# An attention kernel: the adjacency mask is turned by transposing DMA transfers instead of TensorE, and widened by GpSimd instead of ScalarE

## The chip, the cores and the metric

The kernel runs on one core of a Trainium2 chip. The metric is the time of the core on the device in microseconds (us). Three runs of the kernel before are given by their median.

## The reference

One pre-norm graph attention layer with a residual, over 16 batch elements of 512 rows and 512 features, with 16 heads of 32. The mask `adj` is an int32 matrix of zeros and ones per batch element, 512 x 512, mostly zeros.

```python
h = jnp.maximum(_layernorm(x, axis=-1), 0.0)
q, k, v = heads(h @ Wq + bq), heads(h @ Wk + bk), heads(h @ Wv + bv)
scores = jnp.einsum('bhqd,bhkd->bhqk', q, k) * scale
scores = jnp.where(mask[:, None] == 0, -jnp.inf, scores)
attn = jax.nn.softmax(scores, axis=-1)
out = jnp.einsum('bhqk,bhkd->bhqd', attn, v)
x + out.transpose(0, 2, 1, 3).reshape(b, s, D_MODEL) @ Wo + bo
```

## The kernel before

**Two passes over the scores.** For each batch element and head the scores are made twice. Pass 1 has queries on the partitions: TensorE writes a tile of 128 queries x 512 keys (line 822), VectorE adds the mask and takes the row's extreme (608), ScalarE takes the exponential and its sum (444). This gives the softmax's correction c per query. Pass 2 has keys on the partitions: TensorE writes 128 keys x 512 queries with c already inside (834), ScalarE takes the exponential into `probs` (484), then VectorE (622, 625) or GpSimd (359) sets the masked elements to zero, and TensorE multiplies by v (852). A batch element has 64 tiles in either pass: four groups of heads, times four tiles of queries or keys, times four heads.

**The mask in two forms.** `bias_q` has queries on the partitions and holds 0 or -2^100 as bf16; VectorE forms it from `adj_tile`, four tiles per batch element (538). Pass 2 needs the mask with keys on the partitions: `bias_k` (the same numbers, for key tiles 0 and 2) and `keep_k` (int32 one or zero, for key tiles 1 and 3). Each is in two halves, one per pair of key tiles. To get a half, TensorE transposes eight 128x128 pieces of `bias_q` into a PSUM bank (778), and ScalarE copies the first four to `bias_k` (501) and widens the other four to `keep_k` (503). This is the turn called "m".

**The schedule.** Every engine runs the same program of blocks `k`, each of 64 slots `u`. In a slot TensorE does one tile of pass 1 (of block k or k-1), one of pass 2 (tile n = u + 4 of batch element k-1; from u = 60 on, tile u - 60 of batch element k), some of the products of the projections (758), in every fourth slot the product with v, and the turns which the table `TURNS` names: "h" (the transposes of the normalised rows, 772), "c" (783) and "m". Turns and pass-1 tiles share a ring of three PSUM banks, in the order of `RING`; before TensorE writes an entry it waits until the entry that last used this bank has been read. The m turns stand at u = 53 (half 0) and at u = 3 of the next block (half 1).

**SP's queue.** SP issues nearly all DMAs, in program order, each behind its own waits: the loads of x, of adj (`load_adj`, u = 17, 24, 30, 36), of y (the residual's rows) and the stores of y, and `load_stack`: twelve pieces of 32x512 that copy q or k from `part_hi` and `part_lo` into three row ranges of `q_stack` or `k_stack`. The stack loads stand at u = 33, 37, ..., 61 and at u = 1 of the next block; k of group 2 is at u = 49, q of group 3 at u = 61, k of group 3 at u = 1. They are called the k2, q3 and k3 loads here. Behind the k3 load stand, for batch element k-2, the store of y tile 0 (u = 5), the load of y tile 2 into the same buffer (u = 7), which waits for that store, then the store of tile 1 and the load of tile 3.

**GpSimd's program.** It masks tiles 4, 5, 6, 12, 13, 14 and 15 of each group of 16 in pass 2 (359), adds the bias row to the y tiles (350; the third y tile at u = 8, directly behind mask 12 and ahead of masks 13, 14 and 15), and computes the layer norm's scales. The product with v at u = 14 needs tiles 12 to 15 of group 0 masked.

## Time and profile before

| | us |
|---|---|
| median of 3 runs | 1663.86 |
| lowest and highest of them | 1663.39, 1666.87 |
| the profiled execution's own time | 1666.74 |
| its span in the trace | 1664.9 |
| TensorE busy in the span | 1602.4 |
| mean granted TensorE clock | 0.989 of full speed |

The span runs from the first to the last recorded instruction of the profiled execution; its own time is what a run measures. A block lasts about 100 us. The granted clock is given as a share of 2.4 GHz. Times in the timeline are from the span's start.

### The profile page before, as it was taken

Reading aid. Unit: us, or ns where it says so; the run is one execution under the profiler, and the core shown is the slowest. Engines: PE = TensorE matmul, PEld = TensorE weight load, DVE = VectorE, ACT = ScalarE, POOL = GpSimd, SP = SyncE. Lnnn points to the kernel's source line nnn. Section 1 sums busy time; section 2 is a strip of 40 time slices with the busy share of each in tenths; the row PEclk is TensorE's granted clock in tenths of the full one; section 3 lists DMA queues with packets and bytes.
Section 4 is the critical chain, followed back from the end, with each engine's and each line's share of the span. In section 5 each row is a group of like instructions: output and inputs, shape, how many; then the busy total and the mean of one; then the engine's idle time right before and its main releaser. Section 6 shows DMA issues by size and latency. Waiting matters only on the chain.

```text
span 1664.9 us, 27600 instructions
## 1 busy us (share of the span) xinstructions
PE 1602.4 (96%) x7745; PEld 1030.2 (62%) x7745; DVE 1440.1 (86%) x3504; ACT 1457.6 (88%) x3500; POOL 709.9 (43%) x641
## 2 busy tenths in 40 slices
PE   6799999999999999999999999999999999999987
PEld 4556666666666666666666666666666666666643
DVE  4889889888888989889898889989889898888885
ACT  3699899989999989899988998989898989999994
POOL 2044443543443544444453443544443443443442
PEclk9799999999999999999999999999999999999998
DMA  6434343433434344343433434344343434433320
GB/s 208 104 91 114 96 119 87 122 90 114 117 89 126 86 122 115 96 116 90 121 91 116 120 90 120 88 122 112 96 118 84 123 92 118 119 84 104 90 75 26
DMA packets 117168, 175.17 MB, mean 105 GB/s; under 512 B 30861, under 2 KB 32921, under 8 KB 117017
## 3 DMA queue, kind: packets, MB, share of 16 engines
q1 hardware_dynamic: 112536, 171.83, 37.8%
q10 hardware_dynamic: 4480, 1.58, 0.4%
q8 instruction: 64, 1.05, 0.3%
q14 instruction: 88, 0.71, 0.1%
HBM read 54.79 MB, written 16.78 MB: 43 GB/s over the span
## 4 chain that ended last, share of the span: by engine, by line
PE 83%; DVE 6%; ACT 4%; issue 4%; SPq 2%; DMA 1%; ACTq 0%; DVEq 0%
PE psP L758 37%; PE ps L822 16%; PE psO L852 13%; PE ps L834 13%; ACT ps L444 2%; DVE ps L608 2%; SPq L233 2%; PE ps L772 2%; DVE probs L622 1%; PE ps L778 1%; ACT bias_k L501 1%; ACT probs L484 1%; ACT keep_k L503 1%; DVE neg_max L608 0%; DMA q_stack<-part_hi 0%
## 5 line engine op out<-in xcount | busy, mean ns | idle before, releaser
L608 DVE CUSTOM_DVE_ANT_0 ps<-ps,bias_q 128x512 f32<-128x512 f32 x1024 | 708.6, 693 | 174.3 <-PE ps L822 167.1
L359 POOL TENSOR_TENSOR probs<-probs,keep_k 128x512 int32<-128x512 int32 x438 | 565.4, 1311 | 678.3 <-ACT probs L484 676.7
L444 ACT ACTIVATE ps<-ps,neg_max 128x512 f32<-128x512 f32 x1024 | 685.1, 669 | 115.2 <-DVE neg_max L608 92.9
L484 ACT ACTIVATE probs<-ps 128x512 f32<-128x512 f32 x1024 | 618.4, 604 | 16.8 <-PE ps L834 14.2
L822 PE MATMUL ps<-k_stack,q_stack 96*128 96x512 f32 x1024 | 453.2, 443 | 34.9 <-ACT ps L444 29.5
L834 PE MATMUL ps<-q_stack,k_stack 98*128 98x512 f32 x1024 | 411.5, 403 | 6.0 <-ACT probs L484 3.6
L622 DVE SCALAR_TENSOR_TENSOR probs<-bias_k,probs 128x512 f32<-128x512 bf16 x512 | 380.3, 743 | 3.4 <-ACT probs L484 3.2
L822 PEld LDWEIGHTS ps<-k_stack,q_stack 96*128 96x128 f32 x1024 | 193.2, 189 | 300.1 <-ACT ps L444 194.7
L852 PE MATMUL psO<-probs,v_sb 128*32 128x512 f32 x2048 | 275.4, 609 | 4.5 <-ACT probs L484 1.5
L834 PEld LDWEIGHTS ps<-q_stack,k_stack 98*128 98x128 f32 x1024 | 195.6, 191 | 45.3 <-ACT probs L484 17.4
L444 ACT ACTIVATION_READ_ACCUMULATOR ps<-ps,neg_max 128x1 f32 x1024 | 214.5, 210 | 0.0
L608 DVE DVE_READ_ACCUMULATOR2_ANT neg_max<- 128x1 f32 x1024 | 143.6, 140 | 0.0
L336 POOL TENSOR_SCALAR mean_var<-mean_var 128x1 f32<-128x1 f32 x64 | 14.5, 227 | 233.7 <-DVE mean_var L524 233.5
L758 PE MATMUL psP<-wv_hi,hT_hi 128*128 128x512 f32 x256 | 102.2, 399 | 1.1 <-DVE hT_lo L560 1.1
L758 PE MATMUL psP<-hT_hi,wq_hi 128*128 128x512 f32 x256 | 102.4, 400 | 0.7 <-DVE hT_lo L560 0.7
L758 PE MATMUL psP<-hT_lo,wq_hi 128*128 128x512 f32 x256 | 102.2, 399 | 0.0
L758 PE MATMUL psP<-hT_hi,wk_hi 128*128 128x512 f32 x256 | 101.7, 397 | 0.4 <-DVE wk_lo L572 0.3
L758 PE MATMUL psP<-wv_hi,hT_lo 128*128 128x512 f32 x256 | 101.8, 398 | 0.0
L758 PE MATMUL psP<-wv_lo,hT_hi 128*128 128x512 f32 x256 | 101.8, 398 | 0.0
L758 PE MATMUL psP<-hT_hi,wq_lo 128*128 128x512 f32 x256 | 101.7, 397 | 0.0
L852 PEld LDWEIGHTS psO<-probs,v_sb 128*32 128x32 f32 x2048 | 41.4, 108 | 97.2 <-issue 66.5
L758 PE MATMUL psP<-hT_lo,wk_hi 128*128 128x512 f32 x256 | 101.2, 395 | 0.0
(79 smaller groups left out, 1998.3 us busy)
## 6 DMA issues: line engine op xcount, KB each, us to landing
q_stack<-part_hi SPq DMA_DIRECT2D x512, 64.0 KB, 2.0
k_stack<-part_hi SPq DMA_DIRECT2D x504, 64.0 KB, 2.0
x_tile<-in_x_dram SPq DMA_DIRECT2D x66, 256.0 KB, 3.0
adj_tile<-in_adj_dram SPq DMA_DIRECT2D x64, 256.0 KB, 3.0
q_stack<-part_lo SPq DMA_DIRECT2D x256, 64.0 KB, 2.0
k_stack<-part_lo SPq DMA_DIRECT2D x256, 64.0 KB, 2.0
y_tile<-in_x_dram SPq DMA_DIRECT2D x62, 256.0 KB, 2.9
out_dram<-y_tile SPq DMA_DIRECT2D x62, 256.0 KB, 2.1
```

The source lines that it names most:

```text
L233: queue.dma_start(stack[row:row + 32, g, j, :].bitcast(F32), part[32 * j:32 * j + 32, i % 2, :].bitcast(F32)).then_inc(stack_in[kind], 16)
L359: nc.gpsimd.tensor_tensor(bits, bits, keep_k[:, kt // 2, :], ALU.mult).then_inc(gpsimd_masked, 1)
L444: nc.scalar.activation(item, item, ACT.Exp, scale=-1.0, bias=neg_max[:, g % 2, col:col + 1], accum_out=exp_sum[:, col:col + 1]).then_inc(e ...
L484: nc.scalar.activation(probs[:, n % P_RING, :], ps2[:, n % 2, :], ACT.Exp, scale=SCALE).then_inc(exp2_done, 1)
L501: nc.scalar.activation(bias_k[:, n, :], turned[:, 0:S], ACT.Identity).then_inc(bias_k_done, 1)
L608: nc.vector.tensor_tensor_reduce(bank1(("s", u)), bank1(("s", u)), bias_q[:, qt, :], -SCALE, 3.0e38, ALU.add, ALU.min, neg_max[:, g % 2, c ...
L622: nc.vector.scalar_tensor_tensor(out=tile, in0=bias_k[:, kt // 2, :], scalar=-MASKED, in1=tile, op0=ALU.add, op1=ALU.min).then_inc(vector_ ...
L758: last = nc.tensor.matmul(acc, w_l if i == 2 else w_h, m_l if i == 1 else m_h, start=(kt == 0 and i == 0), stop=(kt == NT - 1 and i == 2))
L772: last = nc.tensor.transpose(bank[:, P * t:P * t + P], x_view(b, n)[:, P * t:P * t + P], ident[:])
L822: nc.tensor.matmul(bank1(("s", u)), q_stack[0:STACK, g, j, P * qt:P * qt + P], k_stack[0:STACK, g, j, :], start=True, stop=True).then_inc( ...
L834: nc.tensor.matmul(ps2[:, n % 2, :], k_stack[:, g, j, P * kt:P * kt + P], q_stack[:, g, j, :], start=True, stop=True).then_inc(scores2, 1)
L852: last = nc.tensor.matmul(psO[32 * j:32 * j + 32, :], v_sb[:, (4 * b + kt) % 6, at:at + DH], probs[:, (4 * n + j) % P_RING, :], start=(kt ...
```

## The change

The m turns go. In their place SP issues four transposing DMAs per half (`turn_mask`), at u = 53 for half 0 and u = 61 for half 1: each takes 128 queries x 256 keys of `bias_q` and writes two blocks of 128 keys x 128 queries into the new tensor `turned`. Planes 0 and 1 of `turned` are `bias_k`; planes 2 and 3 share their memory with `adj_tile`, and GpSimd widens them into `keep_k` (`form_keep`, at u = 62 for half 0, at u = 6 of the next block for half 1). The adj loads wait until both widenings before them are done, and the transposes of a half wait until the masks that read the old half are done. The k2 load moves from u = 49 to u = 54, behind the first four transposes. The ring of PSUM banks has 72 entries in place of 74.

```diff
--- before.py
+++ after.py
@@ -46,8 +46,8 @@
 QK_ORDER = [x for x in TILES if x[0] in "qk"]
 
 
-TURNS = {1: [("h", 0, 0)], 3: [("m", 1, -1)], 5: [("h", 1, 0)], 8: [("c", 1, -1)], 10: [("h", 2, 0)], 13: [("h", 3, 0)],
-         24: [("c", 2, -1)], 40: [("c", 3, -1)], 53: [("m", 0, 0)], 56: [("c", 0, 0)]}
+TURNS = {1: [("h", 0, 0)], 5: [("h", 1, 0)], 8: [("c", 1, -1)], 10: [("h", 2, 0)], 13: [("h", 3, 0)],
+         24: [("c", 2, -1)], 40: [("c", 3, -1)], 56: [("c", 0, 0)]}
 
 
 RING = []
@@ -90,9 +90,10 @@
         oT_hi = sb("oT_hi", [P, NT, S], F32R)
         oT_lo = sb("oT_lo", [P, NT, S], F32R)
         x_tile = sb("x_tile", [P, NT, D], F32)
-        adj_tile = sb("adj_tile", [P, S], I32)
+        turned = sb("turned", [P, NT, S], BF16)
+        bias_k = turned[:, 0:2, :]
+        adj_tile = turned[:, 2:4, :].rearrange("p a s -> p (a s)").bitcast(I32)
         bias_q = sb("bias_q", [P, NT, S], BF16)
-        bias_k = sb("bias_k", [P, NT // 2, S], BF16)
         keep_k = sb("keep_k", [P, NT // 2, S], I32)
         probs = sb("probs", [P, P_RING, S], F32)
         part_hi = sb("part_hi", [P, 2, S], F32R)
@@ -138,7 +139,7 @@
         var_done, rstd_done, norm_done = sem("var_done"), sem("rstd_done"), sem("norm_done")
         h_turned, h_hi_done, h_lo_done = sem("h_turned"), sem("h_hi_done"), sem("h_lo_done")
         bias_done = sem("bias_done")
-        m_turned, bias_k_done, m_done = sem("m_turned"), sem("bias_k_done"), sem("m_done")
+        m_in, keep_done = [sem("m_in0"), sem("m_in1")], sem("keep_done")
         qkv_done, out_done = sem("qkv_done"), sem("out_done")
         qk_hi_done, qk_lo_done = sem("qk_hi_done"), sem("qk_lo_done")
         v_done = sem("v_done")
@@ -259,8 +260,20 @@
                     row = 4 * b + t
 
                     sp.wait_ge(bias_done, due(4 * b + t))
-                    sp.dma_start(adj_tile[:], adj_rows[bass.ds(row, 1)].rearrange("a p d -> (a p) d")
+                    sp.wait_ge(keep_done, due(2 * b))
+                    sp.dma_start(adj_tile, adj_rows[bass.ds(row, 1)].rearrange("a p d -> (a p) d")
                                  ).then_inc(adj_in, 16)
+
+            def turn_mask(b, half):
+
+                if have(b):
+                    sp.wait_ge(bias_done, 4 * b + 4)
+                    sp.wait_ge(keep_done, due(2 * b - 1 + half))
+                    sp.wait_ge(vector_masked, due(vector_before(64 * (b - 1) + 48 + 8 * half + 8)))
+                    sp.wait_ge(gpsimd_masked, due(gpsimd_before(64 * (b - 1) + 48 + 8 * half + 8)))
+                    for t in range(NT):
+                        sp.dma_start_transpose(turned[:, half::2, P * t:P * t + P],
+                                               bias_q[:, t, 2 * P * half:2 * P * half + 2 * P]).then_inc(m_in[half], 16)
 
             def load_y(b, t):
                 if have(b):
@@ -293,8 +306,9 @@
                     if u in (7, 11) and k - 2 != LAST: load_y(k - 2, (u + 1) // 4)
                     if u in (44, 46): load_y(k - 1, (u - 44) // 2)
                     if u in (48, 50) and k - 1 == LAST: load_y(LAST, (u - 44) // 2)
-                    if u % 4 == 1:
-                        done = tile_at(k, u // 4 - 1) if u >= 4 else tile_at(k - 1, 15)
+                    if u in (53, 61): turn_mask(k, (u - 53) // 8)
+                    if u % 4 == 1 and u != 49 or u == 54:
+                        done = tile_at(k, u // 4 - 1 - (u == 54)) if u >= 4 else tile_at(k - 1, 15)
                         if done and done[0] in "qk" and done != ("k", 0, 0):
                             load_stack(sp, done[2], QK_ORDER.index(done[:2]))
                         if done == ("k", 0, 0):
@@ -353,13 +367,24 @@
             def mask(b, n):
                 kt = n % 16 // 4
                 if n < 16 and n % 4 == 0:
-                    pool.wait_ge(m_done, due(2 * b + kt // 2 + 1))
+                    pool.wait_ge(keep_done, due(2 * b + kt // 2 + 1))
                 pool.wait_ge(exp2_done, due(64 * b + n + 1))
                 bits = probs[:, n % P_RING, :].bitcast(I32)
                 nc.gpsimd.tensor_tensor(bits, bits, keep_k[:, kt // 2, :], ALU.mult).then_inc(gpsimd_masked, 1)
 
+            def form_keep(b, half):
+
+                if have(b):
+                    pool.wait_ge(m_in[half], 64 * (b + 1))
+                    pool.wait_ge(vector_masked, due(vector_before(64 * (b - 1) + 48 + 8 * half + 8)))
+                    pool.wait_ge(gpsimd_masked, due(gpsimd_before(64 * (b - 1) + 48 + 8 * half + 8)))
+                    nc.gpsimd.tensor_scalar(keep_k[:, half, :], turned[:, 2 + half, :], -1.0 / MASKED, 1.0, ALU.mult, ALU.add
+                                            ).then_inc(keep_done, 1)
+
             def step(k, parity):
                 for u in range(SLOTS):
+                    if u == 62: form_keep(k, 0)
+                    if u == 6: form_keep(k - 1, 1)
                     b, n = pass2(k, u)
                     if have(b) and on_gpsimd(b, n):
                         mask(b, n)
@@ -493,15 +518,6 @@
                                 act.wait_ge(qkv_done, due(12 * k))
                             nc.scalar.activation(hT_hi[:, :, P * n:P * n + P], bank1((kind, n, rel)).rearrange("p (t q) -> p t q", q=P),
                                                  ACT.Relu).then_inc(h_hi_done, 1)
-                        if kind == "m" and have(k + rel):
-                            b = k + rel
-                            act.wait_ge(m_turned, due(2 * b + n + 1))
-                            turned = bank1((kind, n, rel)).bitcast(BF16)
-                            act.wait_ge(vector_masked, due(vector_before(64 * (b - 1) + 48 + 8 * n + 8)))
-                            nc.scalar.activation(bias_k[:, n, :], turned[:, 0:S], ACT.Identity).then_inc(bias_k_done, 1)
-                            act.wait_ge(gpsimd_masked, due(gpsimd_before(64 * (b - 1) + 48 + 8 * n + 8)))
-                            nc.scalar.activation(keep_k[:, n, :], turned[:, S:2 * S], ACT.Identity,
-                                                 scale=-1.0 / MASKED, bias=1.0).then_inc(m_done, 1)
 
             blocks(step, first=0)
 
@@ -532,10 +548,11 @@
             def form_bias(b, t):
 
                 if have(b):
-                    dve.wait_ge(m_turned, due(2 * b))
+                    dve.wait_ge(m_in[0], due(64 * b))
+                    dve.wait_ge(m_in[1], due(64 * b))
                     dve.wait_ge(masked_max, due(64 * (b - 1) + 48 + 4 * t + 4))
                     dve.wait_ge(adj_in, due(16 * (4 * b + t + 1)))
-                    nc.vector.tensor_scalar(bias_q[:, t, :], adj_tile[:], 0.0, MASKED, ALU.is_equal, ALU.mult
+                    nc.vector.tensor_scalar(bias_q[:, t, :], adj_tile, 0.0, MASKED, ALU.is_equal, ALU.mult
                                             ).then_inc(bias_done, 1)
 
             def form_c(b, g):
@@ -613,9 +630,9 @@
 
                         kt = n % 16 // 4
                         if n < 16 and kt % 2 == 0:
-                            dve.wait_ge(bias_k_done, due(2 * b + kt // 2 + 1))
+                            dve.wait_ge(m_in[kt // 2], due(64 * (b + 1)))
                         elif n < 16:
-                            dve.wait_ge(m_done, due(2 * b + kt // 2 + 1))
+                            dve.wait_ge(keep_done, due(2 * b + kt // 2 + 1))
                         dve.wait_ge(exp2_done, due(64 * b + n + 1))
                         tile = probs[:, n % P_RING, :]
                         if kt % 2 == 0:
@@ -711,8 +728,6 @@
                     if kind == "h":
                         pe.wait_ge(h_hi_done, due(4 * b + n + 1))
                         pe.wait_ge(h_lo_done, due(4 * b + n + 1))
-                    elif kind == "m":
-                        pe.wait_ge(m_done, due(2 * b + n + 1))
                     else:
                         pe.wait_ge(c_rows_done, due(4 * b + n + 1))
                     return
@@ -771,13 +786,6 @@
                     for t in range(NT):
                         last = nc.tensor.transpose(bank[:, P * t:P * t + P], x_view(b, n)[:, P * t:P * t + P], ident[:])
                     last.then_inc(h_turned, 1)
-                elif kind == "m":
-                    pe.wait_ge(bias_done, due(4 * b + 4))
-                    for i in range(2 * NT):
-                        key_tile, t = 2 * n + i // NT, i % NT
-                        last = nc.tensor.transpose(bank[:, 64 * i:64 * i + 64].bitcast(BF16),
-                                                   bias_q[:, t, P * key_tile:P * key_tile + P], ident_b)
-                    last.then_inc(m_turned, 1)
                 else:
                     pe.wait_ge(c_lo_done, due(4 * b + n + 1))
                     nc.tensor.transpose(bank[0:32, 0:P], c_parts[:].rearrange("p a n -> p (a n)").bitcast(F32), ident[:]
```

On SP the change adds instructions and moves one load. These are SP's instructions from the load of y tile 1 to the load of y tile 2 in one block, first as they were (`part_hi` and `part_lo` to `k_stack` or `q_stack` are the stack loads, each in twelve pieces; the names in brackets are the semaphores waited on):

```order
L273 DMA y_tile<-in_x_dram 128x512 [waits y_out1]
L233 DMA k_stack<-part_hi 32x512 [waits qk_hi_done,scores2]
...
L233 DMA k_stack<-part_lo 32x512 [waits qk_lo_done]
...
L233 DMA q_stack<-part_hi 32x512 [waits qk_hi_done,scores2]
...
L233 DMA k_stack<-part_hi 32x512 [waits qk_hi_done,scores2]
...
L280 DMA out_dram<-y_tile 128x512 [waits y_done]
L273 DMA y_tile<-in_x_dram 128x512 [waits y_out0]
```

And these are the same now:

```order
L286 DMA y_tile<-in_x_dram 128x512 [waits y_out1]
L275 DMA_TRANSPOSE turned<-bias_q 128x2x128 [waits vector_masked,gpsimd_masked,keep_done,bias_done]
L275 DMA_TRANSPOSE turned<-bias_q 128x2x128 x3
L234 DMA k_stack<-part_hi 32x512 [waits qk_hi_done,scores2]
...
L234 DMA k_stack<-part_lo 32x512 [waits qk_lo_done]
...
L275 DMA_TRANSPOSE turned<-bias_q 128x2x128 [waits vector_masked,gpsimd_masked,keep_done,bias_done]
L275 DMA_TRANSPOSE turned<-bias_q 128x2x128 x3
L234 DMA q_stack<-part_hi 32x512 [waits qk_hi_done,scores2]
...
L234 DMA k_stack<-part_hi 32x512 [waits qk_hi_done,scores2]
...
L293 DMA out_dram<-y_tile 128x512 [waits y_done]
L286 DMA y_tile<-in_x_dram 128x512 [waits y_out0]
```

Four transposes stand ahead of the k2 load and four between it and the q3 load. The k3 load, the store of y tile 0 and the load of y tile 2 follow as before.

GpSimd's instructions around the seam of two blocks, from masks 12 to 15 of the last group on, before:

```order
L359 TENSOR_TENSOR probs<-probs,keep_k 128x512 [waits exp2_done] x4
L359 TENSOR_TENSOR probs<-probs,keep_k 128x512 [waits exp2_done,m_done]
L359 TENSOR_TENSOR probs<-probs,keep_k 128x512 [waits exp2_done] x2
L359 TENSOR_TENSOR probs<-probs,keep_k 128x512 [waits exp2_done,m_done]
L350 TENSOR_TENSOR y_tile<-y_tile,bo_row 128x512 [waits y_in0]
L359 TENSOR_TENSOR probs<-probs,keep_k 128x512 [waits exp2_done] x3
```

And now:

```order
L373 TENSOR_TENSOR probs<-probs,keep_k 128x512 [waits exp2_done] x4
L381 TENSOR_SCALAR keep_k<-turned 128x512 [waits gpsimd_masked,vector_masked,m_in0]
L373 TENSOR_TENSOR probs<-probs,keep_k 128x512 [waits exp2_done,keep_done]
L373 TENSOR_TENSOR probs<-probs,keep_k 128x512 [waits exp2_done] x2
L381 TENSOR_SCALAR keep_k<-turned 128x512 [waits gpsimd_masked,vector_masked,m_in1]
L373 TENSOR_TENSOR probs<-probs,keep_k 128x512 [waits exp2_done,keep_done]
L364 TENSOR_TENSOR y_tile<-y_tile,bo_row 128x512 [waits y_in0]
L373 TENSOR_TENSOR probs<-probs,keep_k 128x512 [waits exp2_done] x3
```

One widening stands ahead of mask 4 and one ahead of mask 12; the addition of the bias row keeps its place.

## Rows read from the trace of the kernel before

**Rows 1.** The page, busy time, share of the span and instructions of each engine.

```profile
PE 1602.4 (96%) x7745; PEld 1030.2 (62%) x7745; DVE 1440.1 (86%) x3504; ACT 1457.6 (88%) x3500; POOL 709.9 (43%) x641
```

**Rows 2.** The page, the chain that ended last, shares by engine.

```profile
PE 83%; DVE 6%; ACT 4%; issue 4%; SPq 2%; DMA 1%; ACTq 0%; DVEq 0%
```

**Rows 3.** Timeline of PE at slot 53: start, length, engine, line, what [idle before].

```profile
960.95 0.63 PE L778 MATMUL ps<-ident,bias_q 128*128 128x128 bf16 x8
961.39 0.48 PE L822 MATMUL ps<-k_stack,q_stack 96*128 96x512 f32 x1
...
962.02 1.06 PE L852 MATMUL psO<-probs,v_sb 128*32 128x512 f32 x8
963.42 0.50 PE L822 MATMUL ps<-k_stack,q_stack 96*128 96x512 f32 x1 [0.34 <-ACT ps L444]
```

**Rows 4.** Timeline of PE, slots 3 and 4 of the next block.

```profile
983.08 0.63 PE L778 MATMUL ps<-ident,bias_q 128*128 128x128 bf16 x8
983.52 0.48 PE L822 MATMUL ps<-k_stack,q_stack 96*128 96x512 f32 x1
...
984.54 0.40 PE L758 MATMUL psP<-wo_hi,oT_lo 128*128 128x512 f32 x1
984.77 0.40 PE L758 MATMUL psP<-wo_hi,oT_hi 128*128 128x512 f32 x1
985.55 0.50 PE L822 MATMUL ps<-k_stack,q_stack 96*128 96x512 f32 x1 [0.38 <-ACT ps L444]
```

**Rows 5.** Timeline of PE, the product with v of slot 14.

```profile
1000.93 1.07 PE L852 MATMUL psO<-probs,v_sb 128*32 128x512 f32 x8
1001.93 0.50 PE L822 MATMUL ps<-k_stack,q_stack 96*128 96x512 f32 x1
```

**Rows 6.** Timeline of POOL: masks 62 and 63, 4 and 5, y tile 2, masks 13-15.

```profile
970.32 2.64 POOL L359 TENSOR_TENSOR probs<-probs,keep_k 128x512 int32<-128x512 int32 x2 [0.82 <-ACT probs L484]
979.14 2.54 POOL L359 TENSOR_TENSOR probs<-probs,keep_k 128x512 int32<-128x512 int32 x2 [6.17 <-ACT probs L484]
...
993.82 1.28 POOL L350 TENSOR_TENSOR y_tile<-y_tile,bo_row 128x512 f32<-128x512 f32 x1 [0.22 <-DMA y_tile<-in_x_dram]
995.05 3.78 POOL L359 TENSOR_TENSOR probs<-probs,keep_k 128x512 int32<-128x512 int32 x3
```

**Rows 7.** Timeline of SP's queue, from the q3 load to y tile 2.

```profile
972.78 2.41 SPq L233 DMA_DIRECT2D q_stack<-part_hi  x4
...
985.37 2.49 SPq L233 DMA_DIRECT2D k_stack<-part_hi  x4
988.02 0.45 SPq L280 DMA_DIRECT2D out_dram<-y_tile  x1
990.20 0.34 SPq L273 DMA_DIRECT2D y_tile<-in_x_dram  x1
```

**Rows 8.** Timeline: VectorE's masks 55 and 0, ScalarE's k3 part.

```profile
959.19 0.69 DVE L625 SCALAR_TENSOR_TENSOR probs<-keep_k,probs 128x512 f32<-128x512 int32 x1
...
973.36 0.69 DVE L622 SCALAR_TENSOR_TENSOR probs<-bias_k,probs 128x512 f32<-128x512 bf16 x1
...
977.80 0.70 ACT L468 ACTIVATE part_hi<-psP,cols 128x512 fp32r<-128x512 f32 x1
```

**Rows 9.** Timeline of PE, the idle that ends at 42.41.

```profile
42.41 0.76 PE L822 MATMUL ps<-k_stack,q_stack 96*128 96x512 f32 x1 [3.82 <-issue]
```

**Rows 10.** Windows of one us: stretch, its length, busy (count) per engine, PEclk, DMA, GB/s.

```profile
42.00:43.00 1.00, 0.59 (x2) 0.53 (x3) 1.00 (x2) 0.00 (x0) 0.00 (x0) 0.71 0.34 59
43.00:44.00 1.00, 1.00 (x4) 0.81 (x3) 1.00 (x1) 0.00 (x0) 0.00 (x0) 0.50 0.79 264
44.00:45.00 1.00, 1.00 (x4) 0.81 (x3) 1.00 (x3) 0.00 (x0) 0.00 (x0) 0.50 0.51 135
45.00:46.00 1.00, 0.73 (x2) 0.01 (x1) 1.00 (x4) 0.27 (x1) 0.00 (x0) 0.59 0.27 66
```

**Rows 11.** DMA issues: target and source, count, KB each, median us to landing.

```profile
k_stack<-part_hi SPq DMA_DIRECT2D x504, 64.0 KB, 2.0
```

## The prediction

> **What bounds the kernel now.** I read the page first: engine totals, clock and chain. TensorE is busy 96% of the span, ScalarE 88%, VectorE 86%, GpSimd 43% [rows 1], and 83% of the chain that ended last is TensorE's own work [rows 2]. So a microsecond taken from TensorE, or a microsecond in which it waits, is one of the result. Work taken from ScalarE counts only where TensorE waits for it.
>
> Then the timeline of one block, k=10, because the schedule repeats every 64 slots. At slot 53 the eight transposes of the mask begin at 960.95 and the next score at 961.39; the score of slot 54 then starts with 0.34 of idle before it, released by the ScalarE exponential that stood behind the two mask copies [rows 3]. The same at slot 3: 983.08 to 983.52, and 0.38 idle before 985.55 [rows 4]. What the reader should see is that a mask turn costs twice: its own time, and a bank that comes free late.
>
> **What the change takes away.** The transposes: 961.39 - 960.95 and 983.52 - 983.08, so 0.44 each. The waits: the rows draw a matmul longer than the step to the next one (984.54 to 984.77 is 0.23 [rows 4]; eight narrow products start 1.00 before their successor, 1000.93 to 1001.93 [rows 5]). So the waits are 985.55 - 984.77 - 0.23 = 0.55 and 963.42 - 962.02 - 1.00 = 0.40. Per batch 0.44 + 0.55 + 0.44 + 0.40 = 1.83, over 16 batches **-29.3 us**. It is an upper end: it holds if ScalarE, freed of two copies per turn, has nothing else behind. The lower end is the transposes alone, 16 x 0.88 = 14.1. I take 29.3, because both rows name ScalarE as the releaser and the copies stand directly before that exponential. The smaller ring (72 entries for 74) changes which bank is used and not how many entries lie between two uses, except at the block's seam, where two become three: nothing, or a little gained.
>
> **What it adds on GpSimd.** 32 widenings. No row shows this form; the nearest are its masks, 2.64 for two [rows 6], so 1.3 each. The first follows mask 63, which ends at 972.96, and the next mask comes at 979.14 after 6.17 of idle; the second stands two slots before mask 12. I cost them at nothing. If that cover were gone, GpSimd's masks would start up to 1.3 later.
>
> **What it adds on SP, the term that decides.** Eight transposing DMAs per batch, four per half. The order matters. The four of the first half stand ahead of the k2 stack load (12 pieces), which moves from slot 49 to 54. The four of the second half stand ahead of the q3 load and, behind it, the k3 load, the store of y tile 0 and the load of y tile 2. All of this is one queue, and it is a full one: from 972.78 to 987.86 SP issues 24 pieces without a gap, 0.63 each; then the store at 988.02 and, when that has landed, the load at 990.20 [rows 7]. GpSimd's addition of the bias row waits for that load (0.22 idle, start 993.82), and masks 13, 14 and 15 stand behind it on GpSimd and end at 998.83 [rows 6]. TensorE's fourth product with v needs all three and starts at 1000.93 [rows 5]. So the slack from SP to TensorE is 1000.93 - 998.83 = 2.1 now, and 1.1 once the turn of slot 3 (0.99) is gone.
>
> Let X be the time for which one transposing DMA holds SP. No row shows one. The lower end is SP's cheapest issue, 0.34 for a load of 128 partitions [rows 7]. The upper end is 2.5: a stack piece, also from SBUF to SBUF, takes 0.63 for 32 partitions, and this one has 128 of them. I take X = 1.0, nearer to the stack piece, since the cost of an issue plainly doesn't follow partitions (the load of 128 is the cheaper of the two), but above it, since a transpose must cut its data into more parts.
>
> The first half may start when mask 55 is done on VectorE, 959.19 + 0.69 = 959.9 [rows 8]; later events move 0.84 forward with the turn of slot 53 gone, so on their clock this is 960.7. Plus 4X is 964.7, plus 12 x 0.63 is 972.2. The second half waits for mask 63 on GpSimd, 970.32 + 2.64 = 972.96 [rows 6], so it isn't late, and q3 starts at 972.96 + 4.0 = 977.0 in place of 972.78: SP is 4.2 later. Nothing in the chain behind it has room, so masks 13 to 15 end at 1003.0, TensorE is ready at 999.9, and it stands still for 4.2 - 1.1 = 3.1. This happens in the 15 blocks that load y tile 2 there: **+46.5 us**.
>
> A stop of this length has a second price. After TensorE's idle of 3.82 before 42.41 the granted clock was 0.71, 0.50, 0.50 and 0.59 in the four microseconds from 42 to 46, half of full speed, the lower of its two levels (1.2 and 2.4 GHz) [rows 9, 10]. The clock lost there is 0.29 + 0.50 + 0.50 + 0.41 = 1.7 us. Between none and 1.7 per stop I take 1.7, because 3.1 is nearer to 3.82 than to the idles of under half a microsecond in rows 3 and 4: **+25.5 us**.
>
> What I cost at nothing: the mask itself is in time. The first half lands at 964.7 + 2.0 (the stack piece's landing [rows 11]), and VectorE first needs it at 973.36 [rows 8]. The second half is issued by 977.0, lands near 979, and is needed after 985.5 [rows 4]. The k2 load lands near 974.2, and ScalarE needs it at 977.80 [rows 8]. The adjacency loads, which now wait for the second widening, come about 15 us later.
>
> **Sum**, against the profiled execution's own time of 1666.7: 1666.7 - 29.3 + 46.5 + 25.5 = 1709.4. The median of the runs is 2.9 lower, so the forecast is **1707**.
>
> A rule speaks against the change. By the table of the Trainium skill, "VectorE: DVE Perf Modes", section "The three transpose paths", one 128x128 bf16 transpose costs 1309 ns by DMA and 390 on TensorE; the trace has eight in 0.44, far below that second figure. If its 1.31 were X, the second half would start at 973.4, q3 at 978.7, the stop would be 4.8, and the time 1666.7 - 29.3 + 15 x 6.5 = 1735, or 1732 against the median.
>
> **Rivals.**
> (a) *A transposing DMA holds SP no longer than a stack piece.* X = 0.63: q3 starts at 975.5, 2.7 late, the stop is 1.6, taken as too short for the clock: 1666.7 - 29.3 + 24 = 1661.4, or 1658.5 against the median, faster. With X = 0.34 the stop is 0.5 and the result 1642. The point from which it decides is where 15 stops equal 29.3, a stop of 1.95, so X = 0.72. For it: issues of 128 partitions at 0.34. Against it: both transfers inside SBUF are the dearer ones. Chance 0.22 for faster, and 0.06 for landing within 0.2% of no change. The Trainium skill says the same in "Advanced Engine Details and Errata", section "X-Bar Transpose (TRN2)": transposing DMAs are as fast as regular ones. No row of this trace shows one.
> (b) *It holds SP longer than 1.2.* Then SP reaches the second half late as well, and each further 0.1 of X costs 0.8. X = 1.5: q3 at 980.3, 7.5 late, a stop of 6.4 plus 1.7, so 1666.7 - 29.3 + 15 x 8.1 = 1759, or 1756 against the median. At 2.5 the stop is 14.4 and the time near 1880. For it: 16-bit elements must be split far finer than rows of 2 KB. Chance 0.17 for an X over 1.3 (above 1732), of it 0.09 above 1756.
> (c) *The stop comes, but the clock holds.* 1666.7 - 29.3 + 46.5 = 1684, or 1681 against the median; 0.2 of the chances, inside those of the forecast's case.
>
> The forecast's case (X from 0.75 to 1.3, with or without the clock) has 0.55. Faster 0.22, within 0.2% (about what a measurement of this kernel can tell from no change) 0.06, slower 0.72. The range goes from 1642, the cheapest issue, to 1756, X = 1.5; about 0.12 is left out. The forecast's case alone would be 1666 to 1732.
>
> **What would show it.** In the timeline of SP: the four transposes' steps (X), q3 starting at about 977 by block 10's clock, no gap from there to the store of y tile 0. In GpSimd's: the addition of the bias row preceded by some 4 us of waiting for the y load, directly before three masks. In TensorE's: no L778, no idle in slots 4 and 54, and one stop of about 3 us before the fourth product with v in each of 15 blocks, with the granted clock at half behind it. The forecast is wrong if X is under 0.72, if the load of y tile 2 isn't what releases the bias row, or if TensorE's wait in slots 4 and 54 stays with the copies gone.

## The result and the profile after

| | before | after |
|---|---|---|
| median of the runs, us | 1663.62 (4 runs) | 1765.58 (4 runs, 1764.79 to 1768.21) |
| ratio | 1 | 1.0614, interval 1.0595 to 1.0633 |
| span of the profiled execution, us | 1664.9 | 1762.9 |

The direction was forecast, the size was not: 1707 was predicted with a range up to 1756, and the change costs 102 us instead of 43. One execution of the kernel of run 9 below took 2376.85 us at a mean granted clock of 0.597 of full speed, and its ratio leaves it out.

The page of the kernel after, first the engines, then the chain that ended last:

```profile
PE 1613.6 (92%) x7489; PEld 1033.1 (59%) x7489; DVE 1456.6 (83%) x3504; ACT 1429.6 (81%) x3436; POOL 738.7 (42%) x673
...
PE 57%; SPq 13%; DVE 11%; DMA 6%; POOL 5%; issue 5%; ACT 3%; ACTq 0%; DVEq 0%
```

TensorE has lost its transposes (7745 instructions [rows 1], now 7489) and is nevertheless busy for longer, 1613.6 instead of 1602.4 us: part of its work now runs at half clock. In the chain its share has gone from 83% [rows 2] to 57%, and SP's queue, DMA and GpSimd have the difference.

The waits of the kernel after, summed over the run (total us, times, longest):

```profile
POOL y_tile L364 <- DMA y_tile<-in_x_dram: 123.6, 28, 9.9
PE psO L860 <- POOL probs L373: 89.9, 15, 9.2
```

TensorE stops 15 times before a product with v and stands still for 89.9 us in all. GpSimd, in turn, stands before the bias-row addition and waits for the y load. Block 10 shows one of the 15. Its slot 0 starts at 1031.72, and at 976.76 before; the times relative to that start can be compared. The timeline of SP:

```profile
1015.11 5.06 SPq L275 DMA_TRANSPOSE turned<-bias_q  x4
1020.27 2.43 SPq L234 DMA_DIRECT2D k_stack<-part_hi  x4
...
1025.35 3.37 SPq L234 DMA_DIRECT2D k_stack<-part_hi  x4
1028.89 5.05 SPq L275 DMA_TRANSPOSE turned<-bias_q  x4
1034.03 2.43 SPq L234 DMA_DIRECT2D q_stack<-part_hi  x4
...
1046.64 2.64 SPq L234 DMA_DIRECT2D k_stack<-part_hi  x4
1049.33 0.58 SPq L293 DMA_DIRECT2D out_dram<-y_tile  x1
1051.63 0.34 SPq L286 DMA_DIRECT2D y_tile<-in_x_dram  x1
```

From the first transpose to the store of y tile 0, over 34 us, SP has no idle of its own. The q3 load starts 2.3 after the block's start; before it was 4.0 ahead of it (972.78 [rows 7] against 976.76), so it is 6.3 later. The y load is issued at 19.9 instead of 13.4. GpSimd:

```profile
1046.02 1.66 POOL L373 TENSOR_TENSOR probs<-probs,keep_k 128x512 int32<-128x512 int32 x1 [7.03 <-ACT probs L509]
1054.65 1.26 POOL L364 TENSOR_TENSOR y_tile<-y_tile,bo_row 128x512 f32<-128x512 f32 x1 [6.97 <-DMA y_tile<-in_x_dram]
1055.87 4.16 POOL L373 TENSOR_TENSOR probs<-probs,keep_k 128x512 int32<-128x512 int32 x3
```

Where the bias row waited 0.22 for the load [rows 6], it waits 6.97, and masks 13 to 15 end at 1060.0. TensorE, and behind it the windows of one microsecond (length, busy share and count of PE, PEld, DVE, ACT, POOL, granted clock, DMA):

```profile
1054.42 0.39 PE L842 MATMUL ps<-q_stack,k_stack 98*128 98x512 f32 x1
1060.17 1.94 PE L860 MATMUL psO<-probs,v_sb 128*32 128x512 f32 x8 [5.36 <-POOL probs L373]
1062.04 0.80 PE L830 MATMUL ps<-k_stack,q_stack 96*128 96x512 f32 x1
```

```profile
1058.00:1059.00 1.00, 0.00 (x0) 0.00 (x0) 1.00 (x2) 0.18 (x2) 1.00 (x2) 1.00 0.93 324
1059.00:1060.00 1.00, 0.00 (x0) 0.00 (x0) 0.50 (x1) 0.00 (x0) 1.00 (x2) 0.53 0.67 152
1060.00:1061.00 1.00, 0.83 (x5) 0.23 (x8) 0.00 (x0) 0.00 (x0) 1.00 (x2) 0.50 0.84 281
...
1065.00:1066.00 1.00, 1.00 (x4) 0.78 (x4) 0.57 (x1) 0.77 (x2) 0.00 (x0) 0.56 0.00 0
1066.00:1067.00 1.00, 1.00 (x6) 0.82 (x5) 0.73 (x3) 1.00 (x3) 0.41 (x1) 1.00 0.00 0
```

The eight narrow products take 1.94 instead of 1.07 [rows 5]. The clock falls while TensorE stands still, and is back after 1065.

**The balance.** Slot by slot (start of a score to start of the next, mean of blocks 2 to 14) a block takes 106.82 us, and 99.89 before. The stop, over the 15 blocks, is 5.99 long and loses 8.04 with the clock behind it (what slots 14 to 18 take beyond their usual lengths): 15 x 8.04 = 120.6. The spans differ by 98.0, so everything else gained 22.6. This is a remainder, and not all of it comes from the turns. Block 2, the first with a stop, starts 3.5 earlier than before (173.7 against 177.2; 176.8 in run 1 below). And from slot 0 of the last batch to the end the kernel takes 96.4 and 90.7 before, 5.7 more, though the stop there is the longest, 9.23, and its slots lose some 10: part of this stop costs nothing.

Without the stop a block gained about 0.9, not 1.83. Slots 3 and 4 fell from 1.91 to 1.47 and from 2.04 to 1.41, as forecast (1.07 together), and 53 and 54 from 1.85 to 1.40 and from 2.04 to 1.55. But slots 50, 55 and 58 rose by 0.35, 0.57 and 0.20 (55: from 1.53 to 2.10) and gave that second half back.

The new instructions (each row: shortest, median and longest in ns):

```profile
L275 SPq DMA_TRANSPOSE turned<-bias_q x128: 1179/1246/2570, 65.4 to 1669.0; - x128
```

```profile
L381 POOL TENSOR_SCALAR keep_k<-turned x32: 620/621/623, 71.8 to 1672.7; 128x512 int32<-128x512 bf16 x32
```

A transpose holds SP for 1.25 us, and a widening takes 0.62.

### The profile page after: what moved, and what is told of

It is laid out like the page before. It is cut to its first block, busy times and chain, and to the rows that moved or that the text cites. A ratio compares the mean times of both kernels' runs of the same rounds, so it can differ in the third digit from the quotient of the medians.

```text
span 1762.9 us, 27359 instructions
## 1 busy us (share of the span) xinstructions
PE 1613.6 (92%) x7489; PEld 1033.1 (59%) x7489; DVE 1456.6 (83%) x3504; ACT 1429.6 (81%) x3436; POOL 738.7 (42%) x673
## 4 chain that ended last, share of the span: by engine, by line
PE 57%; SPq 13%; DVE 11%; DMA 6%; POOL 5%; issue 5%; ACT 3%; ACTq 0%; DVEq 0%
PE psP L773 25%; PE ps L830 11%; PE psO L860 11%; SPq L234 11%; PE ps L842 9%; POOL probs L373 4%; DVE ps L625 3%; DMA y_tile<-in_x_dram 3%; DVE probs L639 3%; DMA out_dram<-y_tile 2%; SPq L275 2%; ACT ps L469 1%; POOL y_tile L364 1%; ACT probs L509 1%; DVE neg_max L625 1%
## 5 line engine op out<-in xcount | busy, mean ns | idle before, releaser
L373 POOL TENSOR_TENSOR probs<-probs,keep_k 128x512 int32<-128x512 int32 x438 | 575.2, 1332 | 625.2 <-ACT probs L509 622.9
L469 ACT ACTIVATE ps<-ps,neg_max 128x512 f32<-128x512 f32 x1024 | 684.6, 669 | 176.8 <-DVE neg_max L625 154.2
L639 DVE SCALAR_TENSOR_TENSOR probs<-turned,probs 128x512 f32<-128x512 bf16 x512 | 393.2, 769 | 2.5 <-ACT probs L509 2.4
L860 PE MATMUL psO<-probs,v_sb 128*32 128x512 f32 x2048 | 286.7, 632 | 95.9 <-POOL probs L373 89.9
L364 POOL TENSOR_TENSOR y_tile<-y_tile,bo_row 128x512 f32<-128x512 f32 x62 | 82.9, 1338 | 123.7 <-DMA y_tile<-in_x_dram 123.6
L350 POOL TENSOR_SCALAR mean_var<-mean_var 128x1 f32<-128x1 f32 x64 | 14.5, 227 | 250.3 <-DVE mean_var L540 249.0
```

What stands on the lines that cost most here:

```text
L364: nc.gpsimd.tensor_tensor(y_view(b, t), y_view(b, t), bo_row[:], ALU.add).then_inc(y_plus_bo, 1)
L373: nc.gpsimd.tensor_tensor(bits, bits, keep_k[:, kt // 2, :], ALU.mult).then_inc(gpsimd_masked, 1)
L469: nc.scalar.activation(item, item, ACT.Exp, scale=-1.0, bias=neg_max[:, g % 2, col:col + 1], accum_out=exp_sum[:, col:col + 1]).then_inc(e ...
L639: nc.vector.scalar_tensor_tensor(out=tile, in0=bias_k[:, kt // 2, :], scalar=-MASKED, in1=tile, op0=ALU.add, op1=ALU.min).then_inc(vector_ ...
L860: last = nc.tensor.matmul(psO[32 * j:32 * j + 32, :], v_sb[:, (4 * b + kt) % 6, at:at + DH], probs[:, (4 * n + j) % P_RING, :], start=(kt ...
```

## The experiments

Three questions: what makes TensorE stop (SP's order, or GpSimd), what a stop costs, and where half of the gain went. All of them start from the kernel after, unless said otherwise.

**1. The k3 load behind the y load.** The total issued on SP stays; only the order changes.

```diff
-                    if u % 4 == 1 and u != 49 or u == 54:
-                        done = tile_at(k, u // 4 - 1 - (u == 54)) if u >= 4 else tile_at(k - 1, 15)
+                    if u % 4 == 1 and u not in (1, 49) or u in (8, 54):
+                        done = tile_at(k - 1, 15) if u == 8 else tile_at(k, u // 4 - 1 - (u == 54))
```

> The k3 stack load moves from slot 1 to slot 8, behind the load of y tile 2; everything else is the changed kernel. Queue theory (the transposes push SP's queue, the late load of y tile 2 holds the bias row on GpSimd and so masks 13 to 15, and TensorE's product with v waits): SP has issued the q3 load 9.8 us into the block, so the store of y tile 0 goes out at 11, the load at 13, it lands at 16.5, the masks end near 22 and TensorE arrives at 23. No stop, no clock fall behind it: 15 times about 7.8 come back, 1640 to 1660 us. GpSimd theory (the widening on GpSimd makes its masks late): the stop stays, over 1740. Landing theory (transposing traffic slows the transfers of y themselves): the load of y tile 2 still takes some 4 us from the store, the stop is shortened by what the earlier start gives.

Measured: 1650.78 (1648.36 to 1654.87) against 1665.29, ratio 0.9923 (0.9895 to 0.9951). SP, GpSimd and TensorE in its block 10, whose slot 0 starts at 970.02:

```profile
980.42 0.55 SPq L293 DMA_DIRECT2D out_dram<-y_tile  x1
982.68 0.34 SPq L286 DMA_DIRECT2D y_tile<-in_x_dram  x1
983.13 3.15 SPq L234 DMA_DIRECT2D k_stack<-part_hi  x4
```

```profile
986.49 1.28 POOL L364 TENSOR_TENSOR y_tile<-y_tile,bo_row 128x512 f32<-128x512 f32 x1 [0.53 <-DMA y_tile<-in_x_dram]
987.73 3.80 POOL L373 TENSOR_TENSOR probs<-probs,keep_k 128x512 int32<-128x512 int32 x3
```

```profile
993.01 1.06 PE L860 MATMUL psO<-probs,v_sb 128*32 128x512 f32 x8
```

The y load is issued 12.7 after the block's start, the bias row waits 0.53, and TensorE doesn't wait. With the transposes in the queue, all of the loss, and the clock's, hung on twelve pieces of k3 standing ahead of the y load. The eight transposes and both widenings are still there, so neither stops TensorE elsewhere (one wait of 1.56 for GpSimd before a product with v is left, in the last batch). What is left is the gain: 14.5 us, by slots 0.86 per block, or 16 x 0.86 = 13.8.

**2. The k2 load back at slot 49**, ahead of the first half's transposes.

```diff
-                    if u % 4 == 1 and u != 49 or u == 54:
-                        done = tile_at(k, u // 4 - 1 - (u == 54)) if u >= 4 else tile_at(k - 1, 15)
+                    if u % 4 == 1:
+                        done = tile_at(k, u // 4 - 1) if u >= 4 else tile_at(k - 1, 15)
```

> The k2 stack load is back at slot 49, as before the change. Queue theory: the second half's transposes then never wait for SP, only for mask 63, so the q3 load starts 1.3 us into the block in place of 1.4 to 2.3; the stop shortens by 0 to 1.0, 1750 to 1766 us. The first half lands about 3 us later and is still in time (it would be needed 3.4 before the block's start and lands at 6 before). If the first half came late there, VectorE would wait for it at slot 61 and the time would rise.

Measured: 1764.33, ratio 1.0602 (1.0571 to 1.0633), an interval that holds the whole of the change's own. The blocks of the profiled executions are 106.20 long for 106.82. Where k2 stands makes no difference that the medians show.

**3. Two transposes in the second half instead of four** from the second batch on. Two of its four query tiles of the turned mask keep the first batch's values. The counts that GpSimd and VectorE wait for are lowered to match; those lines aren't shown, here and in run 4.

```diff
-                    for t in range(NT):
+                    for t in range(2 if half and b else NT):
```

> From the second batch element on, the second half is turned by two transposing DMAs and not four: the masks of queries 256 to 511 for key tiles 2 and 3 are not renewed. Queue theory: SP is 2.5 us earlier for the rest of the block, the stop of 5.4 becomes 2.9. If a stop of 2.9 still makes the clock fall for some 5 us (2.4 lost), 7.8 becomes 5.3 per block: 1728 us. If the clock holds, 1692. GpSimd theory: no change.

Measured: 1732.19 (1725.78 to 1744.18), ratio 1.0418 (1.0369 to 1.0467). That is 33 us for 30 transposes, 1.1 each, near the 1.25 for which each holds SP. The 15 stops fell from 5.99 to 4.28 in the mean, the last batch's from 9.23 to 6.56, and what they lose from 8.04 to about 6.2. The clock fell behind all 15. The time is the expectation's, with the clock falling. (The stops are read in the profiled execution, which took 1744.18, the longest of this kernel.)

**4. One transpose in the second half**; three of its four query tiles are not renewed.

```diff
-                    for t in range(NT):
+                    for t in range(1 if half and b else NT):
```

> As e3_half1_two with one transposing DMA for the second half from the second batch element on: queries 128 to 511 of key tiles 2 and 3 keep an old mask. Idle before TensorE's fourth product with v was 5.75 with four and 4.06 with two (mean of blocks 2 to 14): with one, SP is 1.25 earlier again, an idle of about 2.8. With the clock falling for it (2.0 a stop): 1649 + 15 x 4.8 = 1721. With the clock holding at that length: 1691.

Measured: 1690.82 (1687.0 to 1694.94), ratio 1.0172 (1.0148 to 1.0196). This is the run that prices the clock, because its stops differ in length. Of its 15, ten are 1.13 to 1.78 long and lose the wait and 0.06 to 0.29 more. The other five are 2.14, 3.46, 3.49, 3.76 and 5.11 long and lose 3.70, 5.09, 5.09, 5.24 and 6.82, so 1.5 to 1.7 on top. One of each kind, TensorE's row with the stop ahead of it, and a window behind it:

```profile
911.27 1.07 PE L860 MATMUL psO<-probs,v_sb 128*32 128x512 f32 x8 [3.49 <-POOL probs L373]
...
1113.46 1.06 PE L860 MATMUL psO<-probs,v_sb 128*32 128x512 f32 x8 [1.78 <-POOL probs L373]
```

```profile
913.00:914.00 1.00, 1.00 (x4) 0.81 (x3) 1.00 (x3) 0.83 (x2) 0.00 (x0) 0.50 0.00 0
...
1115.00:1116.00 1.00, 1.00 (x6) 0.80 (x5) 1.00 (x3) 0.78 (x2) 0.00 (x0) 1.00 0.57 207
```

After 3.49 of waiting the clock is 0.50 in the window from 913; after 1.78 it stays at 1.00. The time lies on the branch of the expectation in which the clock holds, because it holds in two stops out of three. That it is met so closely is partly luck: 1691 was worked out for stops of 2.8, and they are 2.18 in the mean.

**5. The bias row behind mask 15.** GpSimd is no longer made to wait ahead of the masks; SP stays late.

```diff
-                    if u == 8 and k - 2 != LAST: add_bo(k - 2, 2)
+                    if u == 11 and k - 2 != LAST: add_bo(k - 2, 2)
```

> On GpSimd the addition of the bias row to y tile 2 stands behind mask 15 (slot 11) and not behind mask 12 (slot 8). Queue theory: SP is as late as in the changed kernel (load of y tile 2 lands 22.9 us into the block), but masks 13 to 15 no longer stand behind it and end near 22, before TensorE arrives. What stays is VectorE's wait for that tile at slot 13, 1 to 2 us, partly hidden: 1650 to 1675 us. If the masks themselves were slow, the stop would stay, over 1740.

Measured: 1694.34 (1688.75 to 1695.91), ratio 1.0177 (1.0142 to 1.0212), a miss. The masks are in time, and the product with v has no wait. But the y load is as late as before, and VectorE needs that tile next. VectorE and TensorE in block 10 of this kernel:

```profile
1016.11 0.69 DVE L668 TENSOR_TENSOR y_tile<-psP,y_tile 128x512 f32<-128x512 f32 x1 [3.16 <-POOL y_tile L364]
...
1017.93 0.68 DVE L577 SCALAR_TENSOR_TENSOR hT_lo<-ps,hT_hi 128x512 fp32r<-128x512 f32 x1
```

```profile
1018.76 0.77 PE L830 MATMUL ps<-k_stack,q_stack 96*128 96x512 f32 x1 [2.48 <-DVE hT_lo L577]
```

The stop moved by two slots and got shorter. Taking one waiter out of a late transfer's way brought out the next; of the edits that keep the whole mask, only the order on SP removes the lateness.

**6. Run 1 with the copies of v tiles 2 and 3 on ScalarE.** The question is the missing half of the gain. In the kernel after, ScalarE's next exponential now waits for VectorE. ScalarE's row, and VectorE's rows up to the maximum that releases it:

```profile
1018.86 0.66 ACT L469 ACTIVATE ps<-ps,neg_max 128x512 f32<-128x512 f32 x1 [1.29 <-DVE neg_max L625]
```

```profile
1016.60 0.68 DVE L673 COPY v_sb<-psP 128x512 f32<-128x512 f32 x1
1017.21 0.68 DVE L537 BATCH_NORM_STATS2 stats<-x_tile 128x6 f32<-128x512 f32 x1
1017.99 0.18 DVE L540 BATCH_NORM_AGGREGATE mean_var<-stats 128x2 f32<-128x6 f32 x1
1018.09 0.67 DVE L625 CUSTOM_DVE_ANT_0 ps<-ps,bias_q 128x512 f32<-128x512 f32 x1
```

The v copy and the statistics (L537, L540) of an x tile stand directly before the row maximum that ScalarE waits for.

```diff
-                        elif kind == "v" and not (b > 0 and n >= 2):
+                        elif kind == "v":
...
-                        elif kind == "v" and b > 0 and n >= 2:
-                            dve.wait_ge(qkv_done, due(qkv_before(b, kind, n) + 1))
-                            dve.wait_ge(pv_done, due(16 * (b - 1) + 12 + n - 1))
-                            nc.vector.tensor_copy(v_sb[:, (4 * b + n) % 6, :], psP[:, T % 2, :]).then_inc(v_done, 1)
```

> The order of SP of e1_k3_behind_y, and the copies of the v tiles 2 and 3 go from VectorE to ScalarE (slots 52 and 56 in place of 53 and 57). The question is why only about half of the forecast gain is there without the stop (99.03 us a block for 99.89, where 1.83 less was forecast): slot 55 lasts 2.10 in place of 1.53 now. VectorE theory (at slots 52 to 55 VectorE is behind with c, the v copy and the statistics, ScalarE waits 1.26 for it at slot 55, and TensorE for ScalarE): 0.6 less on VectorE ahead of slot 55 brings slot 55 back to about 1.6, some 0.5 per block, 1640 to 1645 us. ScalarE theory (ScalarE itself is behind, and the mask copies weren't what it waited for): two more copies on it make slot 55 longer, 1652 or more.

Measured: **1639.77** (1636.91 to 1641.24) against 1661.86, ratio 0.9861 (0.9844 to 0.9877), faster than both kernels. Slot 55 takes 1.52 and slot 58 1.55, and a block 98.16, so 1.73 less than before, where the forecast's two turns came to 1.83. Over 16 blocks that is 27.7; the spans of the profiled executions differ by 26.6 and the medians by 22.1.

**7. Run 1 with VectorE's statistics five slots later** (53 to 58, the two steps behind them along).

```diff
-STATS_AT, RSTD_AT, NORM_AT = (26, 38, 46, 53), (27, 39, 47, 54), (30, 44, 50, 58)
+STATS_AT, RSTD_AT, NORM_AT = (26, 38, 46, 58), (27, 39, 47, 59), (30, 44, 50, 62)
```

> The order of SP of e1_k3_behind_y, and the statistics of the fourth x tile of the next batch element move from slot 53 to 58 (its scale from 54 to 59, its normalisation from 58 to 62), where GpSimd does the masks and VectorE has room. VectorE theory: 0.8 less on VectorE ahead of slot 55, slot 55 back to about 1.55, 1641 to 1645 us. If slot 55 waits for something else: 1651, no change.

Measured: 1651.52 (1649.8 to 1658.3), ratio 0.9942 (0.992 to 0.9964), no better than run 1: a miss, and slot 55 stayed at 2.19. Read alone it would speak against VectorE. GpSimd and VectorE at that place:

```profile
1050.67 1.29 POOL L364 TENSOR_TENSOR y_tile<-y_tile,bo_row 128x512 f32<-128x512 f32 x1
...
1050.86 1.65 DVE L642 SCALAR_TENSOR_TENSOR probs<-keep_k,probs 128x512 f32<-128x512 int32 x1
```

The same mask in run 1, where GpSimd is idle there and makes this addition only at 1055.97, and VectorE beside it:

```profile
1051.16 0.69 DVE L642 SCALAR_TENSOR_TENSOR probs<-keep_k,probs 128x512 f32<-128x512 int32 x1
...
1056.16 0.69 DVE L625 CUSTOM_DVE_ANT_0 ps<-ps,bias_q 128x512 f32<-128x512 f32 x1
...
1056.77 1.16 DVE L639 SCALAR_TENSOR_TENSOR probs<-turned,probs 128x512 f32<-128x512 bf16 x1
```

With the square root's step of the 4th x tile no longer ahead of it, GpSimd's addition comes early and falls on VectorE's mask, which takes 1.62 to 1.67 in all 14 blocks from 1 to 14, and 0.69 in run 1's blocks 2 to 14. The 0.96 that it takes longer is what the edit had freed (the statistics hold VectorE from 1017.21 to 1018.09 in the rows of run 6's question, 0.88). So this run moved one delay and brought another of the same size; it doesn't separate the theories, and run 6 does.

**8. The k3 load late in the kernel before**, as a control: does the order alone gain something?

```diff
-                    if u % 4 == 1:
-                        done = tile_at(k, u // 4 - 1) if u >= 4 else tile_at(k - 1, 15)
+                    if u % 4 == 1 and u != 1 or u == 8:
+                        done = tile_at(k - 1, 15) if u == 8 else tile_at(k, u // 4 - 1)
```

> The kernel before with the one edit of e1_k3_behind_y, the k3 stack load at slot 8 behind the load of y tile 2. It tells whether the gain of that run comes from the order alone. In the kernel before nobody waits on the critical path for that load, so no change: within 2 us of the kernel before. If the order alone gave the gain: 1651.

Measured: 1675.59 (1669.67 to 1680.04), ratio 1.0077 (1.0052 to 1.0103), so it costs 0.8% there, a miss. Slot 18 takes 2.48 instead of 1.68: the store and the load of y tile 3 now stand behind the k3 load. The order helps only where the transposes have made SP late.

**9. The v copies on ScalarE in the kernel before**, the other control (the same edit as in run 6).

> The kernel before (mask turned on TensorE) with nothing changed but the copies of v tiles 2 and 3, moved from VectorE to ScalarE. If VectorE's v copy holds TensorE at slot 55 whatever turns the mask, the time falls as it did in the changed kernel, by 16 x 0.6 to 16 x 0.8, to 1650 to 1654. If the copy only costs where the mask copies are gone from ScalarE (ScalarE is the one that TensorE waits for here, and gets one more copy between two exponentials), the time stays within 0.3% of the kernel before or rises by up to 16 x 0.6 = 10 us.

Measured: 1665.44 against 1664.28, ratio 1.0002 (0.9988 to 1.0016). No gain. Where ScalarE still has the mask copies, slot 54 even rises from 2.04 to 2.11. Run 6's gain therefore needs both: the turn off ScalarE and the copy off VectorE.

**10. Run 6 with the k3 load another four slots later**, at u = 12.

```diff
-                    if u % 4 == 1 and u not in (1, 49) or u in (8, 54):
-                        done = tile_at(k - 1, 15) if u == 8 else tile_at(k, u // 4 - 1 - (u == 54))
+                    if u % 4 == 1 and u not in (1, 49) or u in (12, 54):
+                        done = tile_at(k - 1, 15) if u == 12 else tile_at(k, u // 4 - 1 - (u == 54))
```

> As the best so far (k3 load late, v copies on ScalarE: 1639.8), with the k3 load one step further back, behind the load of y tile 3 instead of ahead of the store and load of y tile 3. If slot 18's excess (1.96 in place of 1.56 us) comes from the load of y tile 3 standing behind the 12 pieces of k3, it goes: 15 x 0.4 = 6, so about 1634. If it comes from something else, the time stays at 1640. If the k3 stack is now late for the scores of slots 19 to 22, the time is above 1640, and TensorE or ScalarE shows idle released by the stack transfer there.

Measured: 1639.01 (1633.91 to 1643.28), ratio 0.9842 (0.9821 to 0.9864). Slot 18 fell from 1.96 to 1.69, as the first branch has it, and slot 50 rose from 2.13 to 2.26; the blocks are 98.06 long for 98.16. The time is that of the second branch, no change: the medians of runs 6 and 10 lie within each other's runs. Slot 50 (1.98 before) was not looked into and stays open.

## Why the prediction was right in direction and wrong in size

The step that failed is the size of the stop, the term of +46.5: it is 5.99 in the mean and not 3.1, so +89.9. The gain (-29.3) was set too high as well, and the clock (+25.5) a little too low.

Right, by its own steps: a queue on SP that is full, with the load of y tile 2 as the item that decides; the bias row released by it; three masks behind it; one stop before the fourth product with v in each of 15 blocks; the clock at half behind it; no loss from the k2 load's place (run 2) nor from the mask's own transfer. The slack was right too: in block 10 TensorE is ready 1.1 earlier in the block (23.1 against 24.2). Run 1 takes this one cause away and with it the whole loss. Rivals (a) and (c) fell: X is far above 0.72, and the clock fell in all 15 stops.

**X was set at 1.0; it is 1.25.** In the forecast's own arithmetic, with rival (b)'s rule above 1.2, q3 comes 4.2 + 0.8 + 0.4 = 5.4 later and the stop is 4.3 long, so X alone is 1.2 of the missing 2.9 per stop. The row for L275 above decides between the two rules weighed. By 1309 ns for one 128x128 transpose (the Trainium skill, "VectorE: DVE Perf Modes", "The three transpose paths") the trace nearly agrees, though one DMA here turns two such blocks. By "as fast as regular DMAs" (the Trainium skill, "Advanced Engine Details and Errata", "X-Bar Transpose (TRN2)"), taken as rival (a) takes it, for the hold on SP, it doesn't: the hold is 1.25 and not 0.63, and the data lands 2.4 after the issue and not 2.0 [rows 11]. The error was in the reason given for 1.0, the nearness to a stack piece, which bounded nothing.

**The queue was taken as free of accidents.** Block 10's q3 starts 6.3 later and not 5.4: the k2 load took 8.5 for its 12 pieces (1020.27 to 1028.72), where 12 x 0.63 = 7.6. Over blocks 2 to 10 the y load is issued at 20.2 in the mean and at 14.0 before. Then the three masks take 4.16 for 3.78 [rows 6]. Together: a stop of 5.36 in block 10, 5.75 in the mean of blocks 2 to 14, and 9.23 in the last batch. The term is +89.9, where +46.5 stood.

**The clock** was priced at 1.7 per stop and costs 8.04 - 5.99 = 2.05: +30.8 for +25.5. Run 4 shows both cases.

**The gain of 29.3 rested on one sentence** that failed: that ScalarE, freed of two copies, has nothing else behind, because the rows name ScalarE as the releaser. The releaser is only the last in a row of them. The gain was 0.9 per block; VectorE came next at slot 55 (ScalarE waits 1.29 for it), and run 6 gets most of the rest by moving the v copy. The lower end given, 14.1, was the better value: run 1 gained 14.5.

**The widenings** at no cost: right, and each takes 0.62 instead of the 1.3 taken from the masks. The adjacency loads don't come 15 later: in block 10 the first is issued 26.4 after slot 0 and 25.9 before, the other three some 7 later, about the length that the stop adds. Nothing in the sum hung on it.

**The sum**, 1666.7 - 22.6 + 89.9 + 30.7 = 1764.7, closes by itself, since 22.6 is a remainder. With the gain of run 1, 14.5, it would be 1772.8, 8 above the profiled execution, and the 3.5 ahead of block 2 and the part of the last stop that costs nothing are of that size.

The range ended at 1756 because X = 1.5 stood for its upper end and every other term kept its middle value. A stop that is a difference of two long chains (20 us of SP's queue against a slack of 1.1) needed the scatter of the queue in the range as well.

## What to carry to other kernels

When work is moved to a DMA queue, list what stands behind it on that queue up to the first item that someone waits for, and ask first whether that item can be put ahead: here one line of order is worth 115 us and turns a loss of 6.1% into a gain of 0.8%. When an engine is freed, read what stands before the next releaser on the other engines before the whole wait is booked as a gain; the wait at one of the two turns had a second owner. And a control in the kernel before tells whether a remedy belongs to the change: both remedies are worth nothing or less without it.

## What was not expected of the hardware

- Two stops of TensorE of nearly the same length cost differently: the 1.78 one of run 4 loses 1.84 and the 2.14 one 3.70. The clock's share does not grow much beyond that (1.7 after the stop of 5.11, 1.2 to 2.9 after those of 5.0 to 9.2 in the kernel after, with the least behind the longest, in the last batch).
- VectorE's masks wait for a GpSimd operation beside them. In the timeline of the kernel before, the 57 masks that begin beside a running mask or addition of GpSimd are 1.25 long in the mean, and the 529 others 0.69; the row maxima, which read the scores from PSUM, are 0.69 in both cases (456 and 568). In run 7's rows VectorE's mask ends 0.55 after GpSimd's addition (1052.51 and 1051.96), near its own 0.69, as if it had only then begun. The Trainium skill has this in "SBUF — State Buffer", section "SBUF: two separate sides": the two engines share a pair of ports under an exclusive lock, and a VectorE operation with two inputs in SBUF and a GpSimd operation that reads SBUF shut each other out for a whole instruction. The rows agree where GpSimd begins first; the other order wasn't looked into.
- A widening from bf16 to int32 on GpSimd takes 0.62, and the int32 product of the same 128x512 elements 1.3.
